# Two graph layers on one core: second-layer weights loaded behind the fifth chunk, two chunks split one to three

## The reference

```python
def layer0(x, adj, w):
    A = adj + eye(4096)
    d = rsqrt(sum(A, axis=1))
    return elu(((A * d[:, None] * d[None, :]) @ x) @ w)

def layer1(x, adj, W, b):
    return relu((adj @ x) @ W.T + b)

x = layernorm(x + layer0(x, adj, w))
x = layernorm(x + layer1(x, adj, W, b))
```

## Time and profile before

| | |
|---|---|
| median of three runs | 867.38 us (866.87 to 867.91) |
| the profiled execution | 869.26 us, of which span 867.3 us |
| PE busy | 792.3 us (91%) |
| PE weight loads | 652.6 us (75%) |
| DVE busy | 745.5 us (86%) |
| ACT busy | 511.8 us (59%) |
| POOL busy | 190.6 us (22%) |
| moved by DMA | 181.71 MB, mean 210 GB/s |

### The profile page before, as it was taken

How to read it: one execution, slowest core, us unless ns; L and a number is a source line. 1 busy time by engine, 2 the same in 40 slices (tenths; PEclk the granted TensorE clock), 3 DMA queues, 4 the chain that set the end, 5 groups by cost and what they waited for, 6 DMA issues and landing times.

```text
span 867.3 us, 10759 instructions
## 1 busy us (share of the span) xinstructions
PE 792.3 (91%) x3532; PEld 652.6 (75%) x3532; DVE 745.5 (86%) x587; ACT 511.8 (59%) x1132; POOL 190.6 (22%) x181
## 2 busy tenths in 40 slices
PE   0465989799999999999999999999999999999996
PEld 0344768578888888888888888888888888888884
DVE  2368979999889999889998999899898998887962
ACT  1355666566776674578776746576744656446351
POOL 0004353351453600012221001020202223023031
PEclk9977989899999999999999999999999999999998
DMA  9999999789999699799989988898997898997400
GB/s 269 320 320 284 216 172 227 180 205 238 254 269 287 144 216 222 210 201 224 212 215 240 208 217 190 188 226 189 211 271 169 205 225 191 213 220 182 102 24 25
DMA packets 183590, 181.71 MB, mean 210 GB/s; under 512 B 6768, under 2 KB 183536, under 8 KB 183536
## 3 DMA queue, kind: packets, MB, share of 16 engines
q1 hardware_dynamic: 94704, 93.21, 46.0%
q10 hardware_dynamic: 88832, 87.83, 42.9%
HBM read 176.82 MB, written 4.19 MB: 209 GB/s over the span
## 4 chain that ended last, share of the span: by engine, by line
PE 62%; DVE 1%; ACT 0%; issue 0%; POOLq 0%; POOL 0%; ACTq 0%; DVEq 0%
PE acc L992 19%; PE acc L994 19%; PE acc L993 19%; PE proj L948 3%; PE proj L946 1%; PE proj L927 0%; ACT acc L481 0%; DVE turned L644 0%; PE acc L969 0%; DVE stats L854 0%; DVE raw L848 0%; PE acc L1025 0%; ACT a_hi L471 0%; DVE v_lo L699 0%; ACT normed L628 0%
## 5 line engine op out<-in xcount | busy, mean ns | idle before, releaser
L992 PE MATMUL acc<-a_hi,v_hi 128*128 128x512 f32 x1024 | 408.9, 399 | 20.5 <-DVE a_lo L659 11.0
L471 ACT ACTIVATE a_hi<-turned 128x1024 fp32r<-128x1024 f32 x256 | 264.4, 1058 | 264.0 <-PE acc L994 134.8
L993 PE MATMUL acc<-a_lo,v_hi 128*128 128x512 f32 x1024 | 403.7, 394 | 0.0
L994 PE MATMUL acc<-a_hi,v_lo 128*128 128x512 f32 x1024 | 403.6, 394 | 0.0
L659 DVE TENSOR_TENSOR a_lo<-turned,a_hi 128x1024 fp32r<-128x1024 f32 x256 | 321.1, 1291 | 32.5 <-ACT a_hi L471 23.4
L644 DVE STREAM_TRANSPOSE turned<-raw 128x2048 f32<-128x2048 f32 x122 | 280.0, 2302 | 6.1
L992 PEld LDWEIGHTS acc<-a_hi,v_hi 128*128 128x128 f32 x1024 | 195.5, 191 | 64.1 <-issue 13.5
L994 PEld LDWEIGHTS acc<-a_hi,v_lo 128*128 128x128 f32 x1024 | 195.3, 191 | 41.6
L993 PEld LDWEIGHTS acc<-a_lo,v_hi 128*128 128x128 f32 x1024 | 195.6, 191 | 40.2
L481 ACT ACTIVATE acc<-raw 128x256 f32<-128x256 f32 x198 | 73.0, 369 | 20.6 <-DMA raw<-in_adj_dram 11.7
L666 DVE TENSOR_REDUCE deg_parts<-raw 128x4 f32<-128x1024 f32 (+3 forms) x29 | 43.0, 1483 | 21.3 <-DMA raw<-in_adj_dram 21.3
(11 more groups left out here) (69 smaller groups left out, 408.2 us busy)
## 6 DMA issues: line engine op xcount, KB each, us to landing
raw<-in_adj_dram SPq DMA_DIRECT2D x154, 512.0 KB, 9.1
raw<-in_adj_dram ACTq DMA_DIRECT2D x154, 512.0 KB, 9.8
x_row<-in_x_dram SPq DMA_DIRECT2D x64, 128.0 KB, 5.4
out_dram<-normed ACTq DMA_DIRECT2D x28, 128.0 KB, 3.3
held<-in_adj_dram ACTq DMA_DIRECT2D x4, 512.0 KB, 13.0
held<-in_adj_dram SPq DMA_DIRECT2D x4, 512.0 KB, 13.0
partial<-in_adj_dram ACTq DMA_DIRECT2D x2, 512.0 KB, 19.0
partial<-in_adj_dram SPq DMA_DIRECT2D x2, 512.0 KB, 18.4
```

The costliest lines, as they stand in the source:

```text
L471: nc.scalar.activation(a_hi[u % 2][:, part, :], turned[u % 2][:, part, :], ACT.Copy).then_inc(s_hi, 1)
L992: pe.matmul(dst, v_hi[:, k, ch], a_hi[u % 2][:, t, :], start=begin, stop=False)
L993: pe.matmul(dst, v_hi[:, k, ch], a_lo[u % 2][:, t, :], start=False, stop=False)
L994: ins = pe.matmul(dst, v_lo[:, k, ch], a_hi[u % 2][:, t, :], start=False, stop=end)
```

## The change

The load of w moves on SP from behind chunk 1 to behind chunk 2 (the third chunk), and gets a semaphore of its own, which `project_x` waits for. The loads of W and b move from behind chunk 1 to behind chunk 4 (the fifth chunk); they come after the wait and the load of x for group 1 that also stand behind chunk 4. PE turns W no longer at its start but when it comes to chunk 4, after the first product and before the turning of x for group 1; it waits for W and b and for the scaled vectors of group 0, since it writes the same PSUM tile. DVE copies the turned W behind its share of chunk 4 instead of chunk 1, and `turn_x` of the later groups waits for that copy. Of chunks 2 and 4 SP issues only part 0 and ACT parts 1, 2 and 3; all other chunks stay at two and two.

```diff
--- before.py
+++ after.py
@@ -230,7 +230,8 @@
         junk = acc[2][:, 1, :].rearrange("p (j m) -> p j m", j=JUNK)
         proj = ctx.enter_context(nc.psum_tensor("proj", [P, GT, C], F32))
 
-        s_w = sem("weights_loaded")
+        s_w = sem("w_loaded")
+        s_wb = sem("second_weights_loaded")
         s_x = sem("x_loaded")
         s_raw = [sem(f"raw_loaded{i}") for i in range(7)]
         s_zero = sem("constants_zeroed")
@@ -294,6 +295,11 @@
             first = PANEL * (group // 2) + STRIPE * q
             return t[first:first + STRIPE, :].rearrange("(t h c) n -> h c t n", h=2, c=B32)[group % 2]
 
+        def parts_of(n, first):
+
+            split = 1 if n in (2, 4) else 2
+            return range(split) if first else range(split, STRIPES)
+
         def load_chunk(eng, n, qs):
             _, row, panel = chunks[n]
             for q in qs:
@@ -360,13 +366,14 @@
             for n in range(len(chunks)):
                 if before[n] is not None:
                     raw_free(sp, before[n])
-                load_chunk(sp, n, (0, 1))
-                if n == 1:
-                    sp.dma_start(w_sb[:], w.rearrange("(h c) n -> c h n", h=CH)).then_inc(s_w, 16)
-                    sp.dma_start(normed[:, 0:CH, :], W.rearrange("(h c) n -> c h n", h=CH)).then_inc(s_w, 16)
-                    sp.dma_start(b_sb[:], b.rearrange("(a n) -> a n", a=1).to_broadcast([P, C])).then_inc(s_w, 16)
+                load_chunk(sp, n, parts_of(n, True))
                 for m in x_loads_after[n]:
                     load_x(m)
+                if n == 2:
+                    sp.dma_start(w_sb[:], w.rearrange("(h c) n -> c h n", h=CH)).then_inc(s_w, 16)
+                if n == PANELS:
+                    sp.dma_start(normed[:, 0:CH, :], W.rearrange("(h c) n -> c h n", h=CH)).then_inc(s_wb, 16)
+                    sp.dma_start(b_sb[:], b.rearrange("(a n) -> a n", a=1).to_broadcast([P, C])).then_inc(s_wb, 16)
             store_last(sp, (0, 1))
             sp.wait_ge(s_out, 16 * (STRIPES * GROUPS + STRIPES))
 
@@ -570,7 +577,7 @@
                 for m in some:
                     if before[m] is not None:
                         raw_free(act, before[m])
-                    load_chunk(act, m, (2, 3))
+                    load_chunk(act, m, parts_of(m, False))
 
             def hi_and_later(u):
 
@@ -579,7 +586,7 @@
                     keep_partial(a)
 
             for n in range(AHEAD):
-                load_chunk(act, n, (2, 3))
+                load_chunk(act, n, parts_of(n, False))
             for n in range(FIRST_B):
                 row, at = divmod(n, PANELS)
                 closing = row < FAST and at == PANELS - 1
@@ -888,14 +895,16 @@
         @block.tensor
         def _(pe):
 
-            pe.wait_ge(s_const, 1)
-            pe.wait_ge(s_w, 48)
-            for h in range(CH):
-                for g in range(CH):
-                    ins = pe.transpose(proj[:, h, P * g:P * (g + 1)], normed[:, g, P * h:P * (h + 1)], ident[:])
-            ins.then_inc(s_wt_mm, 1)
             pe.wait_ge(s_const, 1 + STRIPES)
-            pe.wait_ge(s_wt, 1)
+
+            def turn_second_weights():
+
+                pe.wait_ge(s_wb, 32)
+                pe.wait_ge(s_y, GT)
+                for h in range(CH):
+                    for g in range(CH):
+                        ins = pe.transpose(proj[:, h, P * g:P * (g + 1)], normed[:, g, P * h:P * (h + 1)], ident[:])
+                ins.then_inc(s_wt_mm, 1)
 
             def fold_degrees(row):
 
@@ -912,6 +921,7 @@
                 pe.wait_ge(s_x, 64 * (row + 1))
                 if row:
                     pe.wait_ge(s_y, GT * row)
+                    pe.wait_ge(s_wt, 1)
                 flat = proj[:].rearrange("p t n -> p (t n)")
                 for h in range(CH):
                     for t in range(GT):
@@ -920,6 +930,7 @@
 
             def project_x(row):
 
+                pe.wait_ge(s_w, 16)
                 pe.wait_ge(s_xt, row + 1)
                 flat = x_row[:].rearrange("p t n -> p (t n)")
                 for t in range(GT):
@@ -997,6 +1008,8 @@
 
             for n in range(FIRST_B):
                 row, at = divmod(n, PANELS)
+                if n == PANELS:
+                    turn_second_weights()
                 if row < FAST and at == 1:
                     turn_x(row)
                 if row < FAST and at == 2:
```

## The result

The change makes the kernel slower: 875.69 us (median of three, 873.95 to 877.08) against 867.38 us, a ratio of 1.0103 [1.0076 to 1.0131]. The sign was forecast and the size was not: 8.3 us instead of 3.1. The profiled execution took 877.08 us with a span of 875.3 us, 8.0 us longer than the span before.

What follows compares the result with a forecast made beforehand. PE is full from 200 us, so chunk 7's landing counts: 45.0 + 21.7 + 2.5 + 0.6 = 69.8, 3.1 us later, on the median 867.38 gives 870.5 us. Likeliest case 866.8 to 872.3; 8 in 10: 865.2 to 873.2.

Steps and rivals of the forecast that it cites:

- rival 3: Row 0's closing on DVE is what counts and its 2.8 us carry to the end: 864.6 us; chance 0.10.
- ACT stands in its issues: 12 issues instead of ten before ACT's reduction of chunk 1, which moves from 24.77 to 30.8 us.
- SP's release: SP may issue the second load of x when PE's projection of row 0 ends: 40.1 us instead of 35.57.
- SP's line ends at 36.1 and stands dry until 45: SP's queue up to chunk 4 ends at 36.1 instead of 45.0; x, issued at 40.1, starts only at 45.0.
- Rival 1: SP's dry queue starts x 0.9 us after the issue; chunk 7 lands 0.9 us before today's: 866.5 us; chance 0.20.
- rival 2: SP's dry queue costs nothing, as ACT's moves the whole 347 GB/s meanwhile: -1.4 us, 866.0 us; chance 0.10.
- rival 4: SP's dry queue waits until all of ACT's 14 transfers are through; chunk 7 5.6 us later, 873.0 us; chance 0.10.
- Turning W: PE's transposes and DVE's copy move behind the first product: 1.9 us on PE, covered by its 9.21 us wait.
- x's first packets: Start of the second x load on SP's dry queue: 4.9 us later than at once (4.1 to 5.6), at 45.0.
- x, all four: Second load of x on SP: 3.6 us from today's row plus 0.6 (0 to 1.3) beside a full ACT queue.
- W and b: Their loads on SP, now between x and chunk 5: 2.5 us (2.2 to 2.9) added before chunk 7.
- six transfers of chunks 5 to 7: SP's transfers behind x, W and b up to chunk 7's landing: 3.0 us each, as today.

Runs made afterwards that it cites:

- e1: Kernel before with only the 1:3 split of chunks 2 and 4, w, W and b left behind chunk 1: 868.45 us, median unchanged.
- e2: Changed kernel with all chunks split two and two, so only the move of the weights is left: within 0.2% of the kernel before.
- e7: Kernel before, but POOL's fold of chunk 9 also waits for DVE's low half of unit 2: 865.58 us against 866.08 beside it, ratio 0.9981 to 1.0008.

## Why the prediction was right in sign and wrong in size

**The reading of what bounds the kernel** held for this pair. Row 0's earlier closing led nowhere (rival 3 falls), chunk 7's landing counted, and the shift went through to the end one to one. That it did so is in part luck: both traces happen to have the long stretch behind the sums (41.4 and 41.2 us). Where the stretch differs, as in e1, 4.6 us at the sums are 1.1 at the fold of row 2. The forecast carried chunk 7's shift to the end without a term for this stretch.

**ACT stands in its issues**: forecast 30.8, seen 30.74. The hit is luck. The forecast put the end of the twelfth issue 0.9 us ahead of the eighth landing, at 31.7; that landing came at 29.64, and the issue ended 1.0 us behind it. **L927's first product** (now L938) 34.4, seen 34.30. **SP's release** 40.1, seen 39.86. **Row 0's sums** 41.6, seen 41.06. **SP's line ends at 36.1 and stands dry until 45**: its last packet is at 36.1, its next at 45.6. Rival 1 (the queue starts at once) and rival 2 (nothing lost while one queue works) fall with that row and its 204 GB/s; rival 4 (wait for all of ACT's 14) does not hold either, as ACT's last lands at 49.3 and x starts at 45.6.

**Why one queue alone moves 204 GB/s** the prediction did not show. It took the rate as a property of having one queue, and held it against the rule on issuing engines that it cites. But a queue alone writes one part at a time, that is into one half of the 128 partitions, and two queues that write into the same half move no more (213 GB/s, see the last section). So the 204 GB/s don't refute the rule: whether a queue alone that fills both halves would reach 347 is untested. The loss in the dry stretch is measured either way.

**Turning W**: forecast under 1 us of waiting on PE, seen 2.28, as b landed at 54.6 and not at 51.7. It cost nothing that the trace shows: behind it the projection of row 1 waits 6.08 us for ACT's copy, and PE 9.55 us for the sums.

**The step that failed, and where the other 4.7 us come from** (4.8 by the rounded terms): the step that sizes the way from SP's release to chunk 7. The dry queue was right as the mechanism; four terms of the sum were too small. The measured times of queue starts are first packets, those of transfers landings.

```
term                                  forecast        seen              missing
x's first packets                     45.0            45.6              0.6
x, all four                           3.6 + 0.6       6.1 (to 51.7)     1.9
W and b                               2.5             2.9 (to 54.6)     0.4
six transfers of chunks 5 to 7        6 x 3.0         19.9 (to 74.5)    1.9
```

The first was the dry queue's delay, 5.8 us where I took 4.9 and allowed 5.6. The second is a wrong reading of today's row, in two ways. First, the 3.6 us were no price beside a full ACT queue: ACT's queue was itself silent from 43.9 to 45.1, and x's first three parts landed 0.6 to 0.7 us apart. Beside a busy ACT queue they land 1.2 to 2.0 us apart, with SP's queue dry or not: in e2, never dry, x takes 5.0 us from the landing ahead of it (41.85 to 46.81), and the first load of x took 5.1. That is 0.8 us of the 1.9. Second, I counted x from the landing of the transfer ahead of it (45.0), but with a full line x had begun before that: its first two parts landed at 45.0 and 45.5, beside the last part of chunk 4. A dry queue has no such overlap, and pays the way from the first packet to the first landing (45.6 to 48.0), about 1.1 us more. The fourth came from ACT: its late chunk 5 held back its issue for chunk 9, at 63.49 instead of 57.95, its own queue fell short, and from 67 to 69 the two moved 243 GB/s instead of 347. SP's fifth of the six transfers took 4.7 us (66.7 to 71.4), where the others took 3.0. Here, what was late on one queue came back as a shortage on the other, and this I had not followed at all.

The range for the likeliest case held the six transfers at 3.0 us each and let the other terms vary a little, each by itself. The largest misses, 1.9 us each, are the term that it did not vary and the one that it varied by 0.7.

## What to carry to other kernels

Taking transfers off the longer queue is worth something only if that queue never stands; count for each queue the time until which its line holds work, and put no transfer that needs a release from another engine at its head unless that release comes some 6.5 us before the line ends (9.4 and 5.9 us were enough here, 4.1 and 3.0 were not). Where the order allows it, put a transfer that waits for nobody ahead of it: here that turned +1.0% into -0.5%. Look also at where each queue's transfers land: while both queues write into the same half of the partitions they move some 210 GB/s, and the split here makes them do so. And count a wait for an engine's issues in whatever else this engine does: two more issues on ACT moved its reduction by 6.0 us, and with it what releases SP.

## What was not expected of the hardware

- A transfer given to a queue that was empty, or soon would be, started late beside a full one. These are all stretches up to 130 us in which a queue was silent for over 0.9 us, from the thirteen traces. With three or more of the other queue's transfers still to land, the first packet came 2.7 to 6.6 us after the issue (47 cases); with two or fewer, 1.0 to 1.7 us (21 cases). What decides it is open: it may be the number of packets or of transfers ahead.
- One queue alone moved 200 to 230 GB/s of these 1 KB packets where it had work, two together 347.
- **Two queues moved 347 GB/s together where they wrote into different halves of the 128 partitions, and some 210 where both wrote into the same half.** In all thirteen traces, taken in pieces of 0.5 us from 5 to 97 us, with the packets given to the transfers in the order of issue: where one queue carries part 0 or 1 and the other part 2 or 3, the median is 344 GB/s (1530 pieces); where both are on 0 and 1, or both on 2 and 3, it is 213 (124 pieces). e1 shows it from 36 to 38 us. There SP is at part 0 of chunk 4 and ACT, by the split, at part 1 of the same chunk, and both queues work:

```profile
DMA packets 402, 0.41 MB, mean 206 GB/s; under 512 B 0, under 2 KB 402, under 8 KB 402
...
q1 hardware_dynamic: 200, 0.20, 56.4%
q10 hardware_dynamic: 202, 0.21, 55.1%
```

  This accounts for two slow stretches. From 33 to 37 us the kernels with the split move 211 to 257 GB/s and the kernel before 348; the split gives ACT a part of SP's half. And x's parts 2 and 3 run beside ACT's parts 2 and 3 (233 GB/s from 48 to 52 us after the change, 218 from 46 to 48 us before). That it is the half written, and not something else that goes with the part, is argued: x and adj are different sources, and only the partitions written are shared. A split that keeps the halves apart was not run.
- Still open, too: e1 is 4.6 us late at the sums of row 1 and not slower. 3.4 us come back by the fold of row 2, where the collision on DVE and POOL is missing at the second unit; e7 found no gain from moving that collision alone.
